# Linear attention in front of a mixture-of-experts layer: who turns the rows, who centres them, and the order of a batch's steps

## The chip, the cores and the metric

The kernel runs on one core of one Trainium2 chip. Its metric is the device time in microseconds (us) of one execution. The engines run side by side, each with its own instruction queue, and wait for each other on semaphores: TensorE (PE: products, and transposes by product), VectorE (DVE), ScalarE (ACT), GpSimd (POOL) and SyncE (SP, which here only issues DMAs).

## The reference

The input x holds 16 batches of 1024 tokens of width 256. After a layer norm, two branches are added to x:

```python
xn = _layernorm(x, axis=-1)
Q = _feature_map(xn @ Wq.T + bq)      # elu(t) + 1, 16 heads of 16
K = _feature_map(xn @ Wk.T + bk)
V = xn @ Wv.T + bv
KV = jnp.einsum('bshd,bshe->bhde', K, V)
K_sum = K.sum(axis=1)
Z = 1.0 / (jnp.einsum('bshd,bhd->bsh', Q, K_sum) + 1e-06)
out = jnp.einsum('bshd,bhde,bsh->bshe', Q, KV, Z) @ Wo.T + bo
```

The second branch is an expert layer: softmax gate scores, the best 256 tokens of each batch for each of 8 experts, two products with a gelu between, and the weighted rows added back at their tokens.

## The kernel before

There are two stages. The second, the expert layer (lines 1342 to 1704), is the same in both kernels but for the shape of one helper. The change is in the first, the attention.

**Stage one, batch by batch.** Batch n has 8 tiles j of 128 tokens. DVE takes the statistics (`stats_of`, `moments_of`), POOL adds epsilon and raises to the power -1/2 (`norm`), DVE scales (`root_of`). Each tile is centred into `xm` (`centre`, on DVE, line 899), split into two fp16 halves, a high one on ACT (`high`) and a low one on DVE (`low`), both in `xhl`. The tile must then lie with its width on the partitions: `turn` on PE makes four 128x128 transposes into PSUM (line 1157), and ACT copies them to `xT` (`turn_out`, line 734). `project` is the bias product and six products for K and V into `pP`, then six narrow ones for the gate into `pG`. ACT takes K's negative part, the copy `kv1`, and the exponential `ek`; DVE joins them into `phik`; `sum_kv` adds the tile to the running K-V sums in `pKV`. `q_part` makes a quarter u of the queries; DVE takes its negative part (`q_negative`, line 931), ACT its exponential, and DVE joins them (`q_feature`).

**The second half of a batch's work** comes two batches later, m = n - 2, inside the same eight steps: `blocks_of` on POOL masks the sums by head, `denominators` on PE, then a chain on DVE, `shift` (adds 1e-6), `invert` (a reciprocal and a first bf16 part) and `split_rest` (two more parts, `zpart`); `reciprocals` on PE spreads the parts over four quarters u (line 1233), `divide` on DVE multiplies each with the queries (line 964), `turn_kv` and `fold_o` fold the output weights into `mo`, `output` on PE makes the result (line 1247) and `add_x` on DVE adds it to the rows (line 971) to which POOL has added the output bias (`add_bo`, line 672).

**What sets the order.** No scheduler: each engine's loop body lists, for each step j from 0 to 7, what is issued there, and each queue is taken strictly in that order. On PE:

```python
if j < NT - 1:
    turn(n, j + 1)
...
project(n, j)
...
if j == 3:
    reciprocals(m, 0)
...
    if j > 0:
        sum_kv(n, j - 1)
```

A quarter's product is at steps 4, 5 and 7 and at the end. From batch 5 to 15 DVE also runs the selection of the best 256 tokens for the first four batches, one of three operations over 512 columns at each step (`top_slot`); in batches 0 to 7 it reads four blocks of expert weights for their largest value (`piece`, at odd steps, line 976), which SP loads into `stage`. SP's body issues these loads, the loads of x for two uses (`xring`, `x2ring`), the store of `xhl` into `table`, zeros into `acc` and the stores of the result into `mix`.

After batch 15 a tail finishes batches 14 and 15, and the first gathers of the expert layer are issued.

## Time and profile before

| | us |
|---|---|
| median of 3 runs | 2110.15 |
| lowest and highest | 2107.7, 2118.55 |
| profiled execution, its own time | 2106.6 |
| its span, first to last instruction | 2104.9 |
| first stage to the last tile of batch 15 | about 671 |
| tail between the stages | 42.7 |
| expert layer | 1391.3 |

The profile is one execution. A group of instructions has a line of the kernel, an engine, what it writes and reads, the shape, a count, the busy time, and the idle time before it with what ended it. PE's matmuls are pipelined, so that the durations of neighbours overlap; what one costs its queue is the distance to the next start. The cuts of the stretches below are at the starts of batches 2, 5 and 8 on PE and at the end of batch 15. "PEclk" is the clock granted to TensorE as a share of full speed.

### The profile page before, as it was taken

Reading aid. Unit: us, or ns where it says so; the run is one execution under the profiler, and the core shown is the slowest. Engines: PE = TensorE matmul, PEld = TensorE weight load, DVE = VectorE, ACT = ScalarE, POOL = GpSimd, SP = SyncE. Lnnn points to the kernel's source line nnn. Section 1 sums busy time; section 2 is a strip of 40 time slices with the busy share of each in tenths; the row PEclk is TensorE's granted clock in tenths of the full one; section 3 lists DMA queues with packets and bytes.
Section 4 is the critical chain, followed back from the end, with each engine's and each line's share of the span. In section 5 each row is a group of like instructions: output and inputs, shape, how many; then the busy total and the mean of one; then the engine's idle time right before and its main releaser. Section 6 shows DMA issues by size and latency. Waiting matters only on the chain.

```text
span 2104.9 us, 40792 instructions
## 1 busy us (share of the span) xinstructions
PE 1960.8 (93%) x14240; PEld 1328.3 (63%) x14240; DVE 1392.8 (66%) x2836; ACT 1247.0 (59%) x1975; POOL 881.1 (42%) x776
## 2 busy tenths in 40 slices
PE   4899988898999899999999999999999999999974
PEld 2566656666666566666666666666666666666653
DVE  5877888778786477775567877555555555555535
ACT  3855555566565266566666666666666666666642
POOL 2122112312221356464545554556454545555532
PEclk9999999999999899999999999999999999999987
DMA  5565555334433455555566666666666666666676
GB/s 161 170 200 162 165 176 158 113 124 128 151 131 111 114 121 125 125 125 132 117 160 161 152 172 154 169 153 176 152 166 167 168 165 159 159 168 169 165 181 190
DMA packets 379402, 321.61 MB, mean 153 GB/s; under 512 B 155013, under 2 KB 360842, under 8 KB 379274
## 3 DMA queue, kind: packets, MB, share of 16 engines
q1 hardware_dynamic: 312842, 236.00, 37.5%
q0 software_dynamic: 49152, 67.14, 17.0%
q10 hardware_dynamic: 17280, 16.78, 2.4%
q8 instruction: 78, 1.28, 0.2%
q14 instruction: 50, 0.41, 0.1%
HBM read 185.61 MB, written 100.66 MB: 136 GB/s over the span
## 4 chain that ended last, share of the span: by engine, by line
PE 55%; DMA 3%; POOL 3%; SPq 2%; DVE 2%; issue 1%; ACT 1%; POOLq 0%; ACTq 0%; DVEq 0%
PE pY L1673 27%; PE pH L1659 27%; POOL acc L1499 2%; SPq L223 2%; DMA stage<-in_w 1%; DMA xg<-table,idx 1%; POOL xg L217 1%; DVE yo L1574 1%; DMA lacc<-acc 0%; DVE hid L1561 0%; DMA acc<-yo,idx 0%; DVE w2s L205 0%; ACT hid L1519 0%; ACT w2s L197 0%; ACT gel L1516 0%
## 5 line engine op out<-in xcount | busy, mean ns | idle before, releaser
L1673 PE MATMUL pY<-w2s,hid 128*128 128x256 f16 x6144 | 756.6, 273 | 16.8 <-DVE hid L1561 16.8
L1659 PE MATMUL pH<-xgT,w1s 128*128 128x512 f16 x3072 | 750.3, 381 | 4.3 <-PEq L319 4.3
L1673 PEld LDWEIGHTS pY<-w2s,hid 128*128 128x128 f16 x6144 | 600.3, 98 | 199.9 <-DVE hid L1561 20.8
L1499 POOL DMA_INDIRECT acc<-yo,idx x256 | 415.0, 1621 | 549.3 <-DVE yo L1574 490.8
L1561 DVE SCALAR_TENSOR_TENSOR hid<-gel,cur,hid 128x512 f16<-128x512 f32 x512 | 382.4, 747 | 379.8 <-ACT hid L1519 371.2
L1516 ACT ACTIVATE gel<-pH,cur 128x512 f32<-128x512 f32 x512 | 350.0, 684 | 396.2 <-PE pH L1659 386.5
L1659 PEld LDWEIGHTS pH<-xgT,w1s 128*128 128x128 f16 x3072 | 301.4, 98 | 261.1 <-issue 9.4
L1519 ACT ACTIVATE hid<-gel,cur 128x512 f16<-128x512 f32 x512 | 369.7, 722 | 16.6
L217 POOL DMA_INDIRECT xg<-table,idx x256 | 281.4, 1099 | 113.4 <-issue 60.6
L1169 PE MATMUL pP<-wkv,xT 128*128 128x512 f16 x768 | 190.6, 385 | 0.0
L672 POOL TENSOR_TENSOR x2ring<-x2ring,bo_all 128x512 f32 (+1 forms) x64 | 85.2, 1361 | 151.6 <-DMA x2ring<-in_x 151.5
L205 DVE SCALAR_TENSOR_TENSOR w2s<-stage,cur,w2s 128x1024 f16<-128x1024 f32 x64 | 82.7, 1294 | 82.2 <-ACT w2s L197 82.1
L642 POOL TENSOR_SCALAR veps<-moments 128x8 f32<-128x8 f32 x16 | 3.9, 243 | 314.9 <-DVE moments L836 314.9
L1574 DVE TENSOR_SCALAR yo<-pY,gains,cur 128x256 f32<-128x256 f32 x256 | 121.5, 536 | 13.0 <-PE pY L1673 11.3
L1169 PEld LDWEIGHTS pP<-wkv,xT 128*128 128x128 f16 x768 | 76.4, 99 | 83.6 <-issue 5.4
L1247 PE MATMUL pO<-mo,qz 128*128 128x256 f32 x480 | 117.0, 386 | 6.4 <-DVE qz L964 4.9
L205 DVE SCALAR_TENSOR_TENSOR w1s<-stage,cur,w1s 128x1024 f16<-128x1024 f32 x64 | 82.5, 1290 | 57.9 <-ACT w1s L197 57.8
L773 ACT ACTIVATE ek<-pP,winv_neg 128x256 f32<-128x256 f32 x128 | 59.9, 468 | 90.0 <-PE pP L1169 90.0
L197 ACT ACTIVATE w2s<-stage,cur 128x1024 f16<-128x1024 f32 x64 | 72.8, 1139 | 62.1 <-DMA stage<-in_w 62.0
L734 ACT ACTIVATE xT<-pTK 128x512 f16<-128x512 f16 x128 | 75.8, 592 | 48.7 <-PE pTK L1157 47.2
L1247 PEld LDWEIGHTS pO<-mo,qz 128*128 128x128 f32 x480 | 87.4, 190 | 21.3 <-DVE qz L964 7.9
L1187 PE MATMUL pKV<-kv,phik 128*128 128x129 f32 x512 | 86.9, 293 | 11.5 <-DVE phik L1086 11.5
(185 smaller groups left out, 1995.9 us busy)
## 6 DMA issues: line engine op xcount, KB each, us to landing
stage<-in_w SPq DMA_DIRECT2D x160, 512.0 KB, 5.1
xring<-in_x SPq DMA_DIRECT2D x16, 1024.0 KB, 7.0
x2ring<-in_x SPq DMA_DIRECT2D x16, 1024.0 KB, 9.0
table<-xhl SPq DMA_DIRECT2D x32, 512.0 KB, 3.9
acc<-zeros SPq DMA_DIRECT2D x16, 1024.0 KB, 7.0
mix<-x2ring SPq DMA_DIRECT2D x32, 512.0 KB, 2.8
fmix<-mix SPq DMA_DIRECT2D x48, 256.0 KB, 5.9
facc<-acc SPq DMA_DIRECT2D x48, 256.0 KB, 6.6
```

The lines of the kernel that those rows point to most:

```text
L205: nc.vector.scalar_tensor_tensor(out=part_dst(i, 1, r), in0=staged(r), scalar=cur[i][:, 2 + r // 2:3 + r // 2], in1=part_dst(i, 0, r), op0 ...
L217: nc.gpsimd.indirect_dma_start(xg[i][:, s, :, :, :].rearrange("p a c t -> p (a c t)"), None, table, bass.IndirectOffsetOnAxis(ap=idx[q % 4 ...
L1169: last = t.matmul(pP[j % 2][:, :], xT[h][:, a, c, cols], wkv[:, b, c, :], start=False, stop=k == 2 and c == DC - 1)
L1187: last = t.matmul(pKV[:, c * (P + 1):(c + 1) * (P + 1)], phik[:, j % 2, c * P:(c + 1) * P], kv1[:, j % 2, DC + c, :], start=j == 0 and c = ...
L1247: last = t.matmul(bank[:, i, :], qz[h][:, c, tokens], mo[:, c, :], start=c == 0, stop=c == DC - 1)
L1499: g.indirect_dma_start(acc, bass.IndirectOffsetOnAxis(ap=idx[q][:, s:s + 1], axis=0), yo[i][:, s, :], None, compute_op=ALU.add).then_inc(a ...
L1516: a.activation(gel[:, hc % 2, :], pH[hc % 4][:, :], ACT.Gelu_apprx_tanh, scale=c[:, 0:1]).then_inc(gel_done, 1)
L1519: a.activation(hid[:, hc % 4, 0, :], gel[:, hc % 2, :], ACT.Copy, scale=c[:, 1:2]).then_inc(hhi_done, 1)
L1561: v.scalar_tensor_tensor(out=hid[:, hc % 4, 1, :], in0=gel[:, hc % 2, :], scalar=cur[(q // 2) % 2][:, 1:2], in1=hid[:, hc % 4, 0, :], op0= ...
L1574: last = v.tensor_scalar(yo[i][:, s, :], pY[s // 2][:, s % 2, :], gains[:, ds((b * 4 + q) * 4 + s, 1)], cur[(q // 2) % 2][:, 4:5], ALU.mul ...
L1659: last = t.matmul(pH[hc % 4][:, :], w[:, aw, c, hc * P:(hc + 1) * P], xgT[i][:, ad, c, :], start=k == 0 and c == 0, stop=k == 2 and c == D ...
L1673: last = t.matmul(pY[s // 2][:, s % 2, :], hid[:, hc % 4, ad, s * P:(s + 1) * P], w[:, aw, hc, :], start=hc == 0 and k == 0 and s % 2 == 0 ...
```

## The change

- The rows are turned by SP, with a transposing DMA from `xhl` to `xT` for each tile, in place of PE's four transposes and ACT's copy. It waits for the tile's low half, and at the first tile of a half of the batch for the gate products of the batch before (`gated`), the last readers of that half of `xT`.
- POOL centres the tiles, four `xm` buffers ahead in place of two.
- The gate products of a tile come one step later, the K-V sums two steps behind (`phik` and `kv1` have four buffers).
- The chain of the denominators is spread: `shift` on ACT after step 0, `invert` at step 1 on DVE, `split_rest` at 2, `divide` at 4, 5, 5 and 6; PE has the quarters' products at 2, 3, 6 and 7. The bank that held the transposes, now `pE`, serves the denominators, two of the four quarters of `reciprocals`, and one `output`.
- ACT takes the copies of the sums, of `kvT` and of `dd`, and the queries' negative part, straight from PSUM. The key and query numbers are the same; for the queries the 1 of the feature map is added through the bias and the join is a maximum.
- In the tail, batch 15's chain is taken in between batch 14's output and the weight splits, and the first gathers stand ahead of the last `add_bo`.

```diff
-def turn_probs(pe, k, bank, tiles):
-for t, jl in enumerate(tiles):
-    last = nc.tensor.transpose(bank[0:2 * rows_of(k), t * P:(t + 1) * P], probs[:, jl, lane_cols(k)], ident[:, :])
+def turn_probs(pe, k, bank):
+for jl in range(HALF):
+    last = nc.tensor.transpose(bank[0:2 * rows_of(k), jl * P:(jl + 1) * P], probs[:, jl, lane_cols(k)], ident[:, :])
 last.then_inc(p_turned, 1)
...
-    dve.wait_ge(rows_done, at(rows_done, k + 1))
+    dve.wait_ge(rows_done, at(rows_done, k))
...
-pK = pTK[:, 1, :].bitcast(F32)
+pE = ps("pE", [P, 512])
 pP = [ps(f"pP{i}", [P, 512]) for i in range(2)]
 pG = ps("pG", [P, 2, HALF, 64])
 pKV = ps("pKV", [P, 512])
 pQ = ps("pQ", [P, 512])
...
-banks_z, banks_o, banks_mo = {True: [pD], False: [pD, pKV]}, {True: [pO], False: [pO, pG]}, {True: pD, False: pP[0]}
+banks_z = {True: [pE, pD, pE, pD], False: [pD, pKV, pD, pKV]}
...
+    def turn(n, j):
+        h, jj = divmod(j, HALF)
+        value = held(sp, at(lo_done, n, j))
+        sp.wait_ge(consts, 1)
+        sp.wait_ge(lo_done, value)
+        if jj == 0 and not (isinstance(n, int) and n == 0):
+            value = held(sp, at(gated, n - 1, h))
+            sp.wait_ge(consts, 1)
+            sp.wait_ge(gated, value)
+        sp.dma_start_transpose(
+            xT[h][:, :, :, jj * P:(jj + 1) * P].rearrange("p a c t -> p (a c) t"),
+            xhl[h][:, jj, :, :, :].rearrange("p a c t -> p (a c t)")).then_inc(x_turned[j], 16)
+
...
+    def body(n, s1, s2, load, load2, scan, nxt):
+        m = n - LAG
+        if s1:
+            turn(n, HALF)
+            store_rows(n, 0)
...
         if s1:
+            turn(n, HALF + 1)
+        if load2:
...
+        if s1:
+            turn(n, HALF + 2)
+            turn(n, HALF + 3)
+            store_rows(n, 1)
+        if scan:
+            pieces(n, range(2, PIECES))
+        if nxt:
+            turn(n + 1, 0)
+            turn(n + 1, 1)
+        if s1:
...
+        if nxt:
+            turn(n + 1, 2)
         if s2:
...
+            store_mix(m, 0)
+        if nxt:
+            turn(n + 1, 3)
+        if s2:
+            store_mix(m, 1)
...
+    for j in range(HALF):
+        turn(0, j)
...
+    def centre(n, j):
+        if j == 0:
+            pool.wait_ge(aggr_done, at(aggr_done, n))
+        if n > 0 or j >= HALF:
+            pool.wait_ge(lo_done, at(lo_done, n, j - HALF))
+        g.tensor_scalar(xm[:, j % HALF, :], xring[:, n % XR, j, :], moments[:, j, 0:1], None, ALU.subtract).then_inc(xm_done, 1)
...
+    for n in range(NB):
+        for j in range(HALF, NT):
+            centre(n, j)
+        if n >= LAG:
             for u in range(4):
...
+                add_bo(n - LAG, u)
+        if n < NB - 1:
             norm(n + 1)
...
+            for j in range(HALF):
+                centre(n + 1, j)
+        if n + 1 >= LAG:
+            blocks_of(n + 1 - LAG)
...
-    def turn_out(n, j):
-        h, jj = divmod(j, HALF)
-        act.wait_ge(turned, at(turned, n, j))
-        if jj == 0:
-            act.wait_ge(q_proj, at(q_proj, n, 2 * h + 1 - 4))
-        a.activation(xT[h][:, :, :, jj * P:(jj + 1) * P], pT[:, :, :, :], ACT.Copy).then_inc(xT_done, 1)
-
...
+    def queries(n, u):
         c = u % DC
         act.wait_ge(q_proj, at(q_proj, n, u))
         act.wait_ge(q_done, at(q_done, n, u - 2))
-        a.activation(qraw[:, u % 2, :], banks_q[mixed][u][:, :], ACT.Identity, scale=winv[:, 0:1], bias=bqT[:, c:c + 1]).then_inc(qraw_done, 1)
...
+        a.activation(qraw[:, u % 2, :], pQ[:, :], ACT.Identity, scale=winv[:, 0:1], bias=bqT_one[:, c:c + 1]).then_inc(qraw_done, 1)
         act.wait_ge(qneg_done, at(qneg_done, n, u))
         a.activation(eq[:, u % 2, :], eq[:, u % 2, :], ACT.Exp, scale=-1.0).then_inc(eq_done, 1)
...
+    def sums_out(n):
+        act.wait_ge(kv_used, at(kv_used, n, NT - 1))
+        a.activation(kvring[:, n % QR, :, :].rearrange("p c t -> p (c t)"), pKV[:, 0:DC * (P + 1)], ACT.Copy).then_inc(kv_out, 1)
+
+    def shift(m):
+        act.wait_ge(den, at(den, m))
+        a.activation(dd[:, :], pE[:, 0:P], ACT.Identity, bias=eps[:, 0:1]).then_inc(shifted, 1)
...
+    for n in range(NB):
+        m, s2, nxt = n - LAG, n >= LAG, n < NB - 1
...
+            if j < HALF:
+                high(n, j + HALF)
+            elif nxt and j > HALF:
+                high(n + 1, j - HALF)
+            keys(n, j)
...
+            project(n, j)
+            if j > 0:
+                gate(n, j - 1)
             if s2:
                 if j == 0:
-                    pe.wait_ge(qraw_done, at(qraw_done, n, -2))
                     denominators(m)
...
                     turn_kv(m)
                 if j == 2:
                     fold_o(m)
+            if j in (2, 3):
+                q_part(n, j - 2)
...
+            if s2:
                 if j == 3:
                     reciprocals(m, 0)
                 if j == 4:
                     reciprocals(m, 1)
+                    reciprocals(m, 2)
                 if j == 5:
-                    reciprocals(m, 2)
+                    reciprocals(m, 3)
+                    output(m, 0)
                 if j == 6:
...
+                    output(m, 1)
                 if j == 7:
...
+                    output(m, 2)
+            if n == PREP and j == 6:
...
+                q_part(n, j - 4)
+            if j >= 2:
+                sum_kv(n, j - 2)
+        gate(n, NT - 1)
+        sum_kv(n, NT - 2)
         if s2:
             output(m, 3)
...
+        sum_kv(n, NT - 1)
```

How the order moves, on PE, step 3 and the start of step 4 of a batch (`pP`: K and V of a tile, `pG`: gate, `pKV`: sums, `pQ`: a quarter of the queries, `pTK`: turned rows). Before:

```order
L1157 MATMUL pTK<-ident,xhl 128x128 [waits xT_done,lo_done]
L1157 MATMUL pTK<-ident,xhl 128x128 x3
L1165 MATMUL pP<-bias_rows,bias_lhs 128x512 [waits kv_done,xT_done]
L1169 MATMUL pP<-wkv,xT 128x512 x6
L1176 MATMUL pG<-wg,xT 128x8 x6
L1233 MATMUL pD<-zpart,spread 128x128 [waits zsplit,mo_done]
L1233 MATMUL pD<-zpart,spread 128x128 x11
L1187 MATMUL pKV<-kv,phik 128x129 [waits kv_done,k_done]
L1187 MATMUL pKV<-kv,phik 128x129
```

The same step on PE now, with what follows it in step 4 and the start of step 5:

```order
L1168 MATMUL pP<-bias_rows,bias_lhs 128x512 [waits kv_done,x_turned3]
L1172 MATMUL pP<-wkv,xT 128x512 x6
L1184 MATMUL pG<-wg,xT 128x8 x6
L1209 MATMUL pQ<-xT,wq 128x512 [waits qraw_done]
L1209 MATMUL pQ<-xT,wq 128x512 x5
L1236 MATMUL pE<-zpart,spread 128x128 [waits zsplit]
...
L1236 MATMUL pD<-zpart,spread 128x128 [waits mo_done]
L1236 MATMUL pD<-zpart,spread 128x128 x11
L1236 MATMUL pE<-zpart,spread 128x128 [waits qz_done]
```

The turning is gone from the queue, a quarter of the queries stands ahead of the first spread of the reciprocals, and two further spreads follow at step 4, the second of them waiting for DVE's first `divide`.

On DVE, from the end of step 3 to the first `divide` of step 5, in a batch with selection (`qring`: the joined queries, `qz`: the divided ones). Before:

```order
L964 TENSOR_TENSOR qz<-qring,pD 128x512 [waits bcast]
L1086 SCALAR_TENSOR_TENSOR phik<-kv,ek 128x256 [waits ek_done,kv_used,kv_done]
L892 TENSOR_SCALAR rstd<-rpow 128x8 [waits rpow_done,lo_done]
L906 SCALAR_TENSOR_TENSOR xhl<-xm,rstd,xhl 128x256 [waits hi_done,rstd_done]
L248 MAX_INDEX topu<-topv,rows 64x8 [waits found]
L906 SCALAR_TENSOR_TENSOR xhl<-xm,rstd,xhl 128x256 [waits hi_done]
L899 TENSOR_SCALAR xm<-xring,moments 128x256 [waits lo_done]
L971 TENSOR_TENSOR x2ring<-x2ring,pO 128x512 [waits out_mm,bo_done]
L964 TENSOR_TENSOR qz<-qring,pD 128x512 [waits bcast]
```

The same place on DVE now:

```order
L997 TENSOR_TENSOR qz<-qring,pE 128x512 [waits bcast]
L968 TENSOR_TENSOR qring<-qraw,eq 128x512 [waits eq_done,qraw_done]
L948 TENSOR_REDUCE gmax<-pG 128x4 [waits gated]
L950 TENSOR_TENSOR gsub<-pG,gmax 128x32 [waits gmax_done]
L934 TENSOR_SCALAR rstd<-rpow 128x8 [waits rpow_done,lo_done]
L941 SCALAR_TENSOR_TENSOR xhl<-xm,rstd,xhl 128x256 [waits hi_done,rstd_done]
L248 MAX_INDEX topu<-topv,rows 64x8 [waits found]
L975 SCALAR_TENSOR_TENSOR phik<-kv,ek 128x256 [waits ek_done,kv_used,kv_done]
L997 TENSOR_TENSOR qz<-qring,pD 128x512 [waits bcast]
L997 TENSOR_TENSOR qz<-qring,pE 128x512 [waits bcast]
```

Between the first `divide` and the second there now stand the join of a query quarter, the gate's maximum, the scale of the next batch and a low half that waits for ACT.

On SP, the start of a batch with weight blocks (`stage`). Now (before, `stage` was the first issue of the body, with no wait for a low half):

```order
L526 DMA_TRANSPOSE xT<-xhl 128x4x128 [waits gated,consts]
...
L537 ISA [waits row_out0,consts]
L537 DMA table<-xhl 128x4x512
...
L515 ISA [waits piece_done0,consts]
L515 DMA stage<-in_w 128x1024
...
L566 DMA xring<-in_x 128x8x256
...
L526 DMA_TRANSPOSE xT<-xhl 128x4x128 [waits lo_done,consts]
```

The block's load now stands behind a turn and a store, and both of those behind the low half of tile 4.

## Rows read from the trace of the kernel before

**Rows 1.** The page's first part: engine, busy us (share of the span), instructions.
```profile
PE 1960.8 (93%) x14240; PEld 1328.3 (63%) x14240; DVE 1392.8 (66%) x2836; ACT 1247.0 (59%) x1975; POOL 881.1 (42%) x776
```

**Rows 2.** By stretch: us, each engine's busy us, then PEclk, DMA share, GB/s.
```profile
34.00:92.80 58.80, 51.72 (x386) 30.61 (x384) 44.70 (x131) 45.70 (x97) 11.12 (x13) 1.00 0.49 154
92.80:215.80 123.00, 112.96 (x938) 77.61 (x935) 96.73 (x242) 73.78 (x154) 27.26 (x33) 0.99 0.54 172
215.80:345.70 129.90, 115.60 (x934) 79.37 (x932) 109.02 (x280) 73.66 (x154) 29.02 (x33) 0.96 0.54 171
345.70:671.00 325.30, 299.94 (x2491) 205.48 (x2492) 253.20 (x704) 194.83 (x406) 74.64 (x87) 0.99 0.41 131
671.00:713.70 42.70, 30.77 (x240) 26.07 (x232) 24.83 (x52) 6.17 (x9) 16.40 (x20) 0.83 0.39 117
713.70:2105.00 1391.30, 1345.04 (x9248) 904.97 (x9248) 846.87 (x1379) 846.58 (x1149) 713.36 (x566) 0.98 0.62 155
```

**Rows 3.** PE in order of time, batch 12: start us, us, what [idle before].
```profile
511.14 0.39 PE L1157 MATMUL pTK<-ident,xhl 128*128 128x128 f16 x4
511.36 0.38 PE L1165 MATMUL pP<-bias_rows,bias_lhs 128*128 128x512 f16 x1
...
516.88 0.71 PE L1187 MATMUL pKV<-kv,phik 128*128 128x129 f32 x4 [0.45 <-DVE phik L1086]
...
519.78 1.13 PE L1258 MATMUL pD<-woT,kvT 128*128 128x256 f32 x4 [0.32 <-DVE kvT L1092]
...
525.20 0.83 PE L1233 MATMUL pD<-zpart,spread 128*128 128x128 bf16 x12 [1.98 <-DVE zpart L957]
525.87 0.66 PE L1187 MATMUL pKV<-kv,phik 128*128 128x129 f32 x4
...
528.43 0.31 PE L1176 MATMUL pG<-wg,xT 128*128 128x8 f16 x6 [0.16 <-DVE gsub L915]
...
551.50 0.38 PE L1165 MATMUL pP<-bias_rows,bias_lhs 128*128 128x512 f16 x1
```

**Rows 4.** Waits of PE, 92.8 to 671: total us, times, longest.
```profile
PE pD L1233 <- DVE zpart L957: 30.6, 14, 3.1
```

**Rows 5.** One line of the kernel each: duration ns min/median/max, first and last start.
```profile
L734 ACT ACTIVATE xT<-pTK x128: 573/597/605, 32.7 to 656.3; 128x512 f16<-128x512 f16 x128
...
L899 DVE TENSOR_SCALAR xm<-xring,moments x128: 331/344/1364, 27.6 to 641.5; 128x256 f32<-128x256 f32 x128
...
L906 DVE SCALAR_TENSOR_TENSOR xhl<-xm,rstd,xhl x128: 454/468/1545, 28.9 to 644.7; 128x256 f16<-128x256 f32 x128
...
L964 DVE TENSOR_TENSOR qz<-qring,pD x60: 669/687/690, 106.9 to 701.3; 128x512 f32<-128x512 f32 x60
```

**Rows 6.** Groups by shape, 511.4 to 551.5: busy us, mean ns, idle before.
```profile
L1086 DVE SCALAR_TENSOR_TENSOR phik<-kv,ek 128x256 f32<-128x256 f32 x8 | 3.7, 465 | 2.4 <-ACT ek L782 2.4
...
L937 DVE SCALAR_TENSOR_TENSOR qring<-qraw,eq 128x512 f32<-128x512 f32 x4 | 2.7, 684 | 0.0
...
L740 ACT ACTIVATE qraw<-pQ,bqT,winv 128x512 f32<-128x512 f32 x3 | 2.3, 772 | 0.6 <-PE pQ L1207 0.6
...
L248 DVE FIND_INDEX8 topu<-topv,rows 64x8 uint32<-64x512 f32 x3 | 2.0, 676 | 0.0
...
L915 DVE TENSOR_TENSOR gsub<-pG,gmax 128x32 f32<-128x32 f32 x2 | 0.4, 191 | 0.1
```

**Rows 7.** DVE, then POOL at the same moment, in order of time (batch 6).
```profile
288.81 1.54 DVE L906 SCALAR_TENSOR_TENSOR xhl<-xm,rstd,xhl 128x256 f16<-128x256 f32 x1
...
288.81 5.50 POOL L672 TENSOR_TENSOR x2ring<-x2ring,bo_all 128x512 f32 x4 [14.11 <-DMA x2ring<-in_x]
```

**Rows 8.** Transposing DMAs on SP's queue (ns as in rows 5); a load's landing.
```profile
L223 SPq DMA_TRANSPOSE xgT<-xg x256: 1189/1262/5297, 694.1 to 2033.8; - x128
...
xring<-in_x SPq DMA_DIRECT2D x16, 1024.0 KB, 7.0
```

**Rows 9.** The tail on PE in order of time: start us, us, [idle before].
```profile
694.86 1.61 PE L1258 MATMUL pP<-woT,kvT 128*128 128x256 f32 x4 [3.57 <-DVE kvT L1034]
```

More of the change, by code:

```diff
@@ L433, in block_program @@
             row_out = [event(f"row_out{h}", step=16, credit=1) for h in range(2)]
-            turned = event("turned", per=NT, credit=HALF + 1)
-            xT_done = event("xT_done", per=NT, credit=1)
+            x_turned = [event(f"x_turned{j}", step=16, credit=1) for j in range(NT)]
             proj = event("proj", per=NT)
@@ L970, in add_x @@
                     tiles = x2ring[:, ds(m % 2, 1), 2 * u:2 * u + 2, :].rearrange("p o j d -> p (o j) d")
-                    v.tensor_tensor(tiles, tiles, pair(banks[u % len(banks)]), ALU.add).then_inc(mix_done, 1)
+                    v.tensor_tensor(tiles, tiles, pair(banks_o[not alone][u]), ALU.add).then_inc(mix_done, 1)
                 def piece(n, q):
```

549 lines of the change are left out of this document (238 added, 311 removed).

## The prediction

> **What bounds the kernel now.** I read the page's first part, then the busy time by stretch, then PE in order of time within one batch, then its waits. PE is busy for 93% of the span [rows 1], but the share hides three regimes [rows 2]. The expert layer, 1391.3 us, is not touched, so the change can only work on the first 714 us. There, the first two batches take 58.8 us, batches 2 to 4 take 123.0 (41.0 each), batches 5 to 7 take 129.9 (43.3 each), batches 8 to 15 take 325.3 (40.7 each), and a tail takes 42.7. The reader should see that in batches 5 to 7 DVE is busy for 109.0 of 129.9 us, where the selection and the weight blocks fall together, and in the others for about 78%. So PE bounds most batches, with DVE close behind in three of them.
>
> Batch 12 on PE runs from 511.36 to 551.50, 40.14 us [rows 3]. In it stand four waits with a row, 0.45, 0.32, 1.98 and 0.16, in sum 2.9. The longest is the first spread of the reciprocals, which waits for the last part of the denominator chain on DVE: all 14 batches have it, in sum 30.6 us, up to 3.1 at once [rows 4]. The rest of the batch, 37.2 us, is PE's queue itself.
>
> **The change part by part.**
>
> *Turning leaves PE.* The four transposes of a tile start at 511.14 and the next product at 511.36: 0.22 us of queue [rows 3]. Eight per batch are 1.8 us. What is left of PE's own queue is 37.2 - 1.8 = 35.4 us per batch. No product is added. This is the floor.
>
> *ACT.* It loses eight copies of 0.60 (4.8 us per batch) [rows 5] and gets four more passes over a query quarter at about 0.77 (3.1) [rows 6], plus three copies that DVE had. Its sum hardly moves from 73.8 us in three batches, some 25 each [rows 2], far under 35. At nothing, covered by PE's queue.
>
> *DVE.* It loses eight centrings of 0.34 (2.8) [rows 5], four negative parts and three small copies. With these it falls from 109.0 / 3 = 36.3 us per batch in batches 5 to 7 [rows 2] to about 31, and elsewhere to about 27. It is not the bound by its sum, but it can be by its order.
>
> *The spread chain.* The reciprocals' parts are made at steps 1 and 2 and used at the end of step 3, behind a query quarter: the 1.98 goes. What is late next is the pair of banks. PE puts three spreads close together, and the fourth needs the second `divide`. Between the end of the first `divide` and the end of the second, DVE now has the query join 0.68, three short operations of 0.19, a low half 0.47, a selection step 0.68, a key join 0.47 and the `divide` 0.69 [rows 5, 6]: 3.6 us, and the low half first waits for ACT's high half of the tile, some 0.7 with the two hand-overs, so 4.3. PE in the same time has a spread, 0.67 from start to start [rows 3], K-V sums, a tile's projection and gate: from 525.20 to 528.43 before, less 0.22 of turning, is 3.0. So a new wait of 1.3, and I add 0.5 for the small waits of 0.16 to 0.45 that the order doesn't remove. A batch with selection alone then takes 35.4 + 1.3 + 0.5 = 37.2 us.
>
> In batches 2 to 4 there is no selection step in that list, so the new wait is 0.6; blocks of weights add to DVE elsewhere. I take 37.0. In batches 5 to 7 both are there. A block's reduction at step 3 stands straight ahead of the first `divide`, and that one at step 1 now waits for a load that SP issues only after a turn and a store, where it was first. I take 2 us more than 37.2: 39.2.
>
> *Centring on POOL.* It adds eight operations of 128x256 with one tensor input. No row has such a one. Above it stands POOL's two-input one over 128x512, 5.50 / 4 = 1.37 [rows 7]; below it DVE's own 0.34 [rows 5]. I take 0.7, half of the upper for half the columns. POOL was busy for 27.3 us in three batches [rows 2], 9.1 each, and comes to 15 of 37: no bound, four tiles ahead. Its price is paid on DVE. Where POOL adds the bias, DVE's low half took 1.54 in place of its median 0.47 [rows 5, 7], while `divide`, with one input in PSUM, never took more than 0.69 in 60 [rows 5]. So the operations with two inputs in SBUF wait for POOL. This is in the 0.5 above for the average; the upper bound is a rival.
>
> The Trainium skill has this as a rule ("SBUF — State Buffer", section "SBUF: two separate sides"): a DVE operation with two SBUF inputs and a GpSimd operation that reads SBUF take an exclusive lock on the shared port for a whole instruction. The trace agrees, 1.54 beside 1.37. By it the new centrings, which read SBUF, block as the bias sums do.
>
> *Turning by DMA.* Eight issues per batch on SP, 1.26 us each at the median of the expert layer's, which have the same shape [rows 8]: 10.1 us of SP's queue in 37. SP has otherwise some eight issues a batch; it has room. The trace doesn't show when one lands. Below, it is the issue itself, 1.3 us; above, the issue and a whole 1 MB load in front of it, 7.0 [rows 8], so 8.3, and with two loads in front 15. PE wants a tile about a half batch after its low half, some 18 us, except for tile 3: its low half comes at step 7 and the first query quarter wants it at step 2. Between lie PE's end of the batch and two steps, about 12 us. Only a zero fill and one store stand ahead. At nothing, then, with the upper bound as a rival.
>
> Against this speaks a rule of the Trainium skill ("VectorE: DVE Perf Modes", sections "The three transpose paths" and "Rules for kernel authors"): a 128x128 transpose costs 390 ns on TensorE and 1309 ns by DMA, and TensorE is to be used where PSUM will do. By it a tile of four would take 5.2 us by DMA. The trace differs on both: four in 0.22 us of PE's queue, and an issue for four in 1.26.
>
> *Start.* The first tile could start some 3 us earlier, since four centrings are made at once, but the first weight block now waits behind four turns and holds DVE at step 1. Between 4 us gained and 4 lost I take nothing.
>
> *Tail.* PE waited 3.57 us for a copy of batch 15 that stood behind two weight splits on DVE [rows 9]. ACT has that copy now, and the chain is made earlier. The last bias sums still stand behind eight gathers. I take 4 us of 42.7, between 0 and 8.
>
> **Sum.** Batches 2 to 15 took 123.0 + 129.9 + 325.3 = 578.2. Now 3 x 37.0 + 3 x 39.2 + 8 x 37.2 = 526.2, so 52.0 less, and 4 in the tail: 56. The profiled execution took 2106.6, its span 2104.9, so 2050.6 for it. The median of the runs shown is 3.5 higher. I say 2050. The granted clock was 0.96 to 0.99 in these stretches [rows 2]; what was lost at the lower level after a wait is part of the times before, and I count no further gain for it.
>
> **The rivals.**
>
> *PE's floor is reached.* If DVE's list does not hold up the fourth spread, 14 batches take 35.4: 495.6, a gain of 82.6, and 4: 2020. For it: the waits that I add are made of hand-overs that I only estimate. Against it: DVE's list at step 4 has eight entries, one of them waiting for ACT.
>
> *POOL holds DVE.* Eight more POOL operations per batch fall among twenty DVE ones with two SBUF inputs. If two of them a batch on the way to a `divide` or a key join wait a further 1.1 (1.54 less 0.47), the batches take 2.2 us more, 31 in 14: 2081. For it: the row of 1.54. Against it: most centrings come right after the low half that frees their buffer, while DVE goes on to other work.
>
> *No change.* The order is looser on PE but PE meets new waits at every step, of the sort between 0.3 and 0.5: 4 us a batch give back all, 2106. Only if several at once.
>
> *Transposes land late, slower.* Tile 3's must land 12 us after its low half. If DMAs with 512 small rows wait in their rings behind zeros, a store, `table` and `xring`, and SP stands at the store of the result until DVE has added it, each batch waits for what exceeds 12 us. It decides from 4 us beyond, where the 3.7 us gained per batch are gone; at 18 us after the low half, 6 us of wait, the 14 batches come out 2.3 us longer each: 2106.6 + 32 - 4 = 2135. For it: the longest of the 256 issues took 5.3 us [rows 8]. Against it: the DMA share is 0.54 and 0.41 [rows 2].
>
> **How the numbers follow.** A measurement of this kernel can tell some 0.5% from no change, 10.5 us. The forecast has 0.50, by itself 2038 to 2066; PE's floor 0.20; POOL 0.18; no change 0.06; late transposes 0.06. That leaves out a range from 2022 to 2088 hardly more than the last two and a part of the floor. Faster by more than 0.5%: 0.50 + 0.20 + 0.18 and a part of the rest, 0.89; the same 0.06; slower 0.05.
>
> **What would show it.** PE's first product of a batch should come every 37 us, 39 in batches 5 to 7. The first spread should have no wait for the last denominator part, and the fourth one about 1.3 for `divide`. No wait of PE for a transposing DMA beyond the first batches, and issues of about 1.26 on SP. POOL's centrings between 0.34 and 1.37, and DVE's low halves in two groups, near 0.47 and above 1. The tail should have no 3.57 before its fold. The forecast is wrong if PE's waits name DMAs, if DVE is busy for over 90% of a batch, or if the expert layer moves from 1391.3 us.

## The result, and the profile after

The changed kernel takes 2033.1 us at the median of four runs (2030.8 to 2034.3), beside 2112.6 for the kernel before in runs on the same chip: 0.962 of it, 95% interval 0.959 to 0.965. I had said 2050, between 2022 and 2088. The profiled execution's span went from 2104.9 to 2032.5 us, 72.4 less.

The page's first part, as in [rows 1]:

```profile
PE 1913.8 (94%) x13728; PEld 1289.4 (63%) x13728; DVE 1311.2 (65%) x2598; ACT 1229.0 (60%) x1959; POOL 1025.3 (50%) x904
```

The stretches of [rows 2], cut at the same batches (the columns are those of [rows 2]):

```profile
31.40:89.60 58.20, 51.19 (x320) 28.20 (x321) 37.46 (x112) 43.79 (x93) 28.97 (x32) 0.90 0.89 222
89.60:199.90 110.30, 105.09 (x841) 70.98 (x840) 80.46 (x193) 70.52 (x151) 56.67 (x61) 1.00 0.84 226
199.90:317.40 117.50, 105.99 (x837) 71.37 (x835) 94.20 (x236) 70.25 (x150) 56.51 (x58) 0.99 0.78 215
317.40:600.90 283.50, 277.18 (x2254) 189.34 (x2255) 216.04 (x590) 184.85 (x396) 141.85 (x144) 1.00 0.64 177
600.90:636.60 35.70, 25.36 (x232) 21.30 (x221) 21.56 (x44) 7.04 (x12) 16.67 (x20) 1.00 0.48 148
636.60:2032.50 1395.90, 1345.48 (x9248) 904.92 (x9248) 847.27 (x1379) 846.69 (x1149) 711.40 (x565) 0.98 0.63 154
```

| stretch | before | after | gain | forecast |
|---|---|---|---|---|
| batches 0 and 1, with the start | 92.8 | 89.6 | 3.2 | 0 |
| batches 2 to 4 | 123.0 | 110.3 | 12.7 | 12.0 |
| batches 5 to 7 | 129.9 | 117.5 | 12.4 | 12.3 |
| batches 8 to 15 | 325.3 | 283.5 | 41.8 | 27.7 |
| tail | 42.7 | 35.7 | 7.0 | 4 |
| expert layer | 1391.3 | 1395.9 | -4.6 | 0 |

Batch 12 on PE, in order of time, beside [rows 3]:

```profile
460.13 0.38 PE L1168 MATMUL pP<-bias_rows,bias_lhs 128*128 128x512 f16 x1
...
470.70 1.46 PE L1209 MATMUL pQ<-xT,wq 128*128 128x512 f16 x6
471.99 0.83 PE L1236 MATMUL pE<-zpart,spread 128*128 128x128 bf16 x12
...
475.49 0.83 PE L1236 MATMUL pE<-zpart,spread 128*128 128x128 bf16 x12
...
478.18 0.29 PE L1184 MATMUL pG<-wg,xT 128*128 128x8 f16 x6
479.13 0.84 PE L1236 MATMUL pD<-zpart,spread 128*128 128x128 bf16 x12 [0.66 <-DVE qz L997]
...
495.32 0.38 PE L1168 MATMUL pP<-bias_rows,bias_lhs 128*128 128x512 f16 x1
```

The batch takes 35.19 us in place of 40.14. The first spread has no wait. A single one is left, 0.66 us ahead of the fourth. DVE around it, from the first `divide` to the second:

```profile
473.41 0.67 DVE L997 TENSOR_TENSOR qz<-qring,pE 128x512 f32<-128x512 f32 x1
474.36 0.69 DVE L968 TENSOR_TENSOR qring<-qraw,eq 128x512 f32<-128x512 f32 x1 [0.27 <-ACT eq L782]
...
476.74 0.74 DVE L941 SCALAR_TENSOR_TENSOR xhl<-xm,rstd,xhl 128x256 f16<-128x256 f32 x1 [1.24 <-ACT xhl L762]
...
477.48 0.68 DVE L248 FIND_INDEX8 topu<-topv,rows 64x8 uint32<-64x512 f32 x1
478.08 0.40 DVE L975 SCALAR_TENSOR_TENSOR phik<-kv,ek 128x256 f32<-128x256 f32 x1
478.40 0.67 DVE L997 TENSOR_TENSOR qz<-qring,pD 128x512 f32<-128x512 f32 x1
```

The first `divide` ends at 474.08, the second at 479.07, and the spread starts at 479.13. PE's waits from batch 1 to the end of batch 15, beside [rows 4] (total us, times, longest):

```profile
PE pE L1236 <- DVE qz L997: 11.6, 7, 2.5
PE pD L1236 <- DVE qz L997: 7.1, 10, 1.3
PE pKV L1195 <- DVE phik L975: 4.2, 3, 2.8
PE pE L1236 <- DVE zpart L991: 3.5, 4, 1.2
```

The 30.6 us for `zpart` have become 3.5; waits for `qz`, the divided queries, have come, 18.7 us in all. What had no row before are POOL's centring and SP's turns (ns as in [rows 5]):

```profile
L683 POOL TENSOR_SCALAR xm<-xring,moments x128: 914/925/1481, 26.3 to 560.4; 128x256 f32<-128x256 f32 x128
```

```profile
L526 SPq DMA_TRANSPOSE xT<-xhl x128: 1188/1197/3917, 28.6 to 577.3; - x128
...
  PE pP L1168: 21.7, 2
...
DMA to landing us min/median/max: 2.4/4.0/9.6
```

PE waited for a turned tile twice: 18.9 us at the very start, where it has nothing else to do, and 2.76 us in batch 0. DVE, from the start of the first batch to the end of batch 15, waited for the weight blocks (total us, times, longest):

```profile
DVE piece_max L1008 <- DMA stage<-in_w: 35.7, 13, 5.4
```

### The profile page after: what moved, and what is told of

The parts are those of the page before. It is cut to its first block, busy times and chain, and to the rows that moved or that the text cites. A ratio compares the mean times of both kernels' runs of the same rounds, so it can differ in the third digit from the quotient of the medians.

```text
span 2032.5 us, 39422 instructions
## 1 busy us (share of the span) xinstructions
PE 1913.8 (94%) x13728; PEld 1289.4 (63%) x13728; DVE 1311.2 (65%) x2598; ACT 1229.0 (60%) x1959; POOL 1025.3 (50%) x904
## 4 chain that ended last, share of the span: by engine, by line
PE 56%; DMA 3%; POOL 3%; issue 2%; DVE 2%; SPq 2%; ACT 1%; POOLq 0%; ACTq 0%; DVEq 0%
PE pY L1674 28%; PE pH L1660 28%; POOL acc L1500 2%; SPq L223 2%; DMA stage<-in_w 2%; DMA xg<-table,idx 1%; POOL xg L217 1%; DVE yo L1575 1%; DVE hid L1562 0%; DMA acc<-yo,idx 0%; ACT hid L1520 0%; DVE lmix L1593 0%; ACT gel L1517 0%; DMA lacc<-acc 0%; POOL idx L212 0%
## 5 line engine op out<-in xcount | busy, mean ns | idle before, releaser
L1674 PE MATMUL pY<-w2s,hid 128*128 128x256 f16 x6144 | 757.2, 273 | 22.0 <-DVE hid L1562 18.7
L683 POOL TENSOR_SCALAR xm<-xring,moments 128x256 f32<-128x256 f32 x128 | 130.6, 1031 | 82.4 <-DVE xhl L941 75.4
L1575 DVE TENSOR_SCALAR yo<-pY,gains,cur 128x256 f32<-128x256 f32 x256 | 121.5, 536 | 12.7 <-PE pY L1674 11.0
L197 ACT ACTIVATE w1s<-stage,cur 128x1024 f16<-128x1024 f32 x64 | 72.9, 1140 | 51.0 <-DMA stage<-in_w 50.8
L673 POOL TENSOR_SCALAR veps<-moments 128x8 f32<-128x8 f32 x16 | 12.9, 807 | 175.9 <-DVE moments L875 175.9
L941 DVE SCALAR_TENSOR_TENSOR xhl<-xm,rstd,xhl 128x256 f16<-128x256 f32 x128 | 63.5, 496 | 58.1 <-ACT xhl L762 58.1
L1209 PE MATMUL pQ<-xT,wq 128*128 128x512 f16 x384 | 93.3, 379 | 0.8 <-ACT qraw L780 0.8
L712 POOL TENSOR_TENSOR x2ring<-x2ring,bo_all 128x512 f32<-128x512 f32 x64 | 88.5, 1413 | 5.0 <-DMA x2ring<-in_x 5.0
```

The source lines that it names most:

```text
L197: nc.scalar.activation(part_dst(i, 0, r), staged(r), ACT.Copy, scale=cur[i][:, 2 + r // 2:3 + r // 2]).then_inc(whi_done, 1)
L683: g.tensor_scalar(xm[:, j % HALF, :], xring[:, n % XR, j, :], moments[:, j, 0:1], None, ALU.subtract).then_inc(xm_done, 1)
L1575: last = v.tensor_scalar(yo[i][:, s, :], pY[s // 2][:, s % 2, :], gains[:, ds((b * 4 + q) * 4 + s, 1)], cur[(q // 2) % 2][:, 4:5], ALU.mul ...
L1674: last = t.matmul(pY[s // 2][:, s % 2, :], hid[:, hc % 4, ad, s * P:(s + 1) * P], w[:, aw, hc, :], start=hc == 0 and k == 0 and s % 2 == 0 ...
```

## The experiments

"2 to 4" and "5 to 7" are us per batch, "12" is batch 12, each from the profiled execution, from PE's first product of a batch to that of the next. The ratio is to runs of the kernel before on the same chip, whose medians were 2108.7 to 2112.6; so two kernels measured on different chips can differ by some 4 us for that alone.

| kernel | median us | ratio, 95% interval | 2 to 4 | 5 to 7 | 12 |
|---|---|---|---|---|---|
| before | 2112.6 | | 41.0 | 43.3 | 40.1 |
| after | 2033.1 | 0.962 (0.959 to 0.965) | 36.8 | 39.2 | 35.19 |
| turn_only | 2135.2 | 1.013 (1.011 to 1.014) | 45.8 | 45.5 | 40.6 |
| turn_clear | 2100.9 | 0.996 (0.994 to 0.998) | 41.6 | 42.4 | 40.7 |
| chain_late | 2041.8 | 0.969 (0.968 to 0.971) | 38.3 | 40.7 | 35.18 |
| late_swap | 2053.8 | 0.973 (0.970 to 0.976) | 40.9 | 42.3 | 35.23 |
| one_behind | 2053.9 | 0.975 (0.973 to 0.976) | 38.7 | 39.2 | 36.10 |
| centre_dve | 2038.9 | 0.967 (0.965 to 0.970) | 37.8 | 39.4 | 35.00 |
| centre_twice | 2054.4 | 0.975 (0.972 to 0.977) | 37.0 | 39.5 | 35.75 |
| pieces_first | 2010.5 | 0.954 (0.950 to 0.958) | 34.5 | 36.4 | 35.19 |
| picks_moved | 2026.6 | 0.961 (0.958 to 0.964) | 36.4 | 38.9 | 34.37 |
| first_moved | 2003.1 | 0.949 (0.947 to 0.952) | 34.6 | 35.8 | 34.37 |
| both | 2014.0 | 0.954 (0.951 to 0.956) | 34.6 | 36.3 | 34.37 |
| scales_late | 2006.1 | 0.952 (0.950 to 0.954) | 34.5 | 35.7 | 34.37 |

**turn_only: the turning alone, in the kernel before.**

```diff
-                                turn(n, j + 1)
...
-                                turn_out(n, j + 1)
...
+                    if s1:
+                        turn(n, HALF)
+                        store_rows(n, 0)
                     if scan:
                         pieces(n, range(2))
...
-                pe.wait_ge(xT_done, at(xT_done, n, j))
+                pe.wait_ge(x_turned[j], at(x_turned[j], n))
```

> The kernel before, with the turning alone taken over by SP's transposing DMA (PE's four transposes and ACT's copy gone, nothing else moved). My theory: PE's queue loses 0.22 us at each of 128 tiles, 28 us in all, but the three of them that stand between the denominators and the first spread only lengthen the wait for the last denominator part, which DVE's chain sets, and batches 5 to 7 are held by DVE. So 1.1 us per batch in 13 batches and nothing in three: about 2098 us beside 2113, and PE's wait for zpart grows from 30.6 to some 38 us. Rival 1, turning is worth its whole queue: 28 us, 2084. Rival 2, the transposing DMAs land late where SP has other loads: PE waits for x_turned and the time stays at 2113 or rises.

It was slower, by 26 us. PE did not wait for turned tiles beyond the start (rival 2 names the wrong wait); its waits for `zpart` went to 55.6 us. DVE in batch 4, then PE's wait over the first stage:

```profile
198.99 0.42 DVE L1116 COPY kvT<-pD 128x256 f32<-128x256 f32 x1
203.93 1.22 DVE L1000 TENSOR_REDUCE piece_max<-stage 128x1 f32<-128x1024 f32 x1 [4.53 <-DMA stage<-in_w]
...
207.52 0.92 DVE L971 RECIPROCAL zz<-dd 128x128 f32<-128x128 f32 x1
```

```profile
PE pD L1248 <- DVE zpart L981: 55.6, 13, 7.4
```

The weight block's load stood behind a turn on SP, the block's reduction waited for it, and the chain of the denominators stands behind the reduction. In batch 12 there are no blocks, the turns' 1.8 us are gone from the queue, and nothing is gained (40.6 in place of 40.1). PE there:

```profile
557.22 0.83 PE L1248 MATMUL pD<-zpart,spread 128*128 128x128 bf16 x12 [2.20 <-DVE zpart L981]
...
558.65 2.77 PE L1184 MATMUL pP<-wkv,xT 128*128 128x512 f16 x6
```

The wait is 2.20 in place of 1.98, and the six products behind it take 2.77 us; the clock granted over this batch is 0.96 of full speed, a part of it at the lower level (1.2 of 2.4 GHz). In batch 12 of the kernel before they took 1.46 in this place:

```profile
526.81 1.46 PE L1169 MATMUL pP<-wkv,xT 128*128 128x512 f16 x6
```

**turn_clear: turn_only with the loads first.**

```diff
+                    if scan:
+                        pieces(n, range(2))
                     if s1:
                         turn(n, HALF)
                         store_rows(n, 0)
-                    if scan:
-                        pieces(n, range(2))
```

> The kernel before with DMA turning alone, as in turn_only, but SP issues the first two weight blocks of a batch ahead of the turn of tile 4 and the store, as the kernel before did. My theory: turn_only came out 26 us above before because in batches 0 to 7 block 0's load stood behind that turn, so that DVE waited up to 5.4 us for it at step 1, ahead of the denominator chain (PE's wait for zpart went to 6 to 7 us a batch). With the load first these waits go, some 4 to 5 us in each of six batches: 2105 to 2111 us, batches 2 to 4 at 40 to 41.5 and not 45.8, and PE's longest wait for zpart at 3 to 4 us. Rival: it is the turning itself (late landings, or a lower clock after each longer wait) that costs it: then the time stays above 2125.

```profile
91.90:216.70 124.80, 110.89 (x840) 73.50 (x839) 97.34 (x243) 61.22 (x130) 27.27 (x33) 0.96 0.69 199
```

34 us back, and 4 us under the lowest that I expected: batches 2 to 4 took 137.5 in turn_only. The cause of turn_only's loss is the load, not the turning. Turning alone in the kernel before is worth 8 us, 0.4%, and not the 28 of its queue, and in the profiles batches 2 to 15 give only 1.8 of it (577.8 and 576.0 us). The traces show where the queue time went: PE's listed waits there grew from some 49 to 63 us, the one for `zpart` from 30.6 to 34.1, and PE ran for longer at the lower clock (0.96, 0.95 and 0.97 granted in batches 2 to 4, 5 to 7 and 8 to 15, beside 0.99, 0.96 and 0.99 [rows 2]). Two neighbouring batches of turn_clear, 11 and 12, wait the same 2.20 us at the first spread:

```profile
469.23:508.80 39.57, 35.25 (x281) 23.73 (x279) 32.61 (x90) 20.27 (x44) 9.45 (x11) 1.00 0.59 160
508.80:549.48 40.68, 36.76 (x281) 24.36 (x279) 32.45 (x90) 20.38 (x44) 9.46 (x11) 0.96 0.53 156
```

The second had a stretch at the lower clock (mean 0.96), and took 1.1 us longer. No run puts the turning back on PE in the changed kernel, where little waiting is left to cover it; what it is worth there was not measured.

**chain_late: the chain in one piece at step 3.**

```diff
-                        if s2 and j == 1:
-                            invert(m)
...
-                            if j == 2:
+                            if j == 3:
+                                invert(m)
                                 split_rest(m)
```

> The changed kernel with the denominator chain not spread: the reciprocal and the two further parts both at DVE's step 3, in place of steps 1 and 2. My theory: the first spread waits for zpart again, by 1.5 to 2.5 us in each of 14 batches: 2054 to 2068 us beside 2033, and the wait for zpart stands in PE's list with 20 to 35 us. Rival: the query quarter that now stands ahead of the first spread (2 us of PE's queue) covers it, less than 0.5 us per batch, up to 2040; then the spreading as such was worth little and the order on PE did it.

8.7 us slower, less than I gave it, and all of it in batches 2 to 7. In batch 12 the last part starts on DVE and the first spread on PE here:

```profile
479.19 0.29 DVE L991 TENSOR_TENSOR zpart<-zrest,zpart 128x128 bf16<-128x128 f32 x1
```

```profile
480.51 0.83 PE L1235 MATMUL pE<-zpart,spread 128*128 128x128 bf16 x12
```

It is ready at 479.48, 1.0 us early. The quarter ahead of the spread, 1.3 us of queue, covers it. The rival holds for batches 8 to 15.

**late_swap: chain_late, and the first spread ahead of the quarter.**

```diff
-                        if j in (2, 3):
-                            q_part(n, j - 2)
+                        if j == 2:
+                            q_part(n, 0)
...
                             if j == 3:
                                 reciprocals(m, 0)
...
+                        if j == 3:
+                            q_part(n, 1)
```

> The changed kernel with the denominator chain not spread (as in chain_late) and, on PE at step 3, the first spread ahead of the query quarter. chain_late showed the last denominator part ready 1.0 us before the first spread in batch 12; the quarter is 1.3 us of queue. My theory: the two edits cover each other; without both the first spread waits again, by 0.3 us in batches 8 to 15 and by 1.3 us more than in chain_late in batches 2 to 7: about 2053 us. Rival 1: a clock drop behind the new wait or a knock-on adds to it, 1 us more a batch, above 2060. Rival 2: the wait only changes place (the quarter stood still behind the divide), 2042 as chain_late.

2053.8, as expected, with PE's wait for `zpart` back (batches 1 to 15):

```profile
PE pE L1235 <- DVE zpart L991: 33.4, 13, 5.5
```

But in batch 12 that wait is only 0.20 us, and the batch takes 35.23. So most of the 1.98 of [rows 3] went there with neither the spreading nor the quarter. What is left as its cause is DVE's shorter list and the rest of the new order; that is argued, and no run separates them.

**one_behind: the K-V sums one step behind.**

```diff
-                        if j >= 2:
-                            sum_kv(n, j - 2)
+                        if j >= 1:
+                            sum_kv(n, j - 1)
                     gate(n, NT - 1)
-                    sum_kv(n, NT - 2)
```

> The changed kernel with the K-V sums one step behind in place of two. My theory: the sum of a tile then meets phik half a microsecond early at most steps, as it did before the change (0.45 us in one step of batch 12), 0.5 to 1.5 us per batch: 2041 to 2055 us beside 2033. Rival: a tile's product with a gate and a quarter between give ACT and DVE time enough at each step, no wait for phik of over 0.2 us, 2033.

21 us slower, at the far end of what I expected. PE's waits for `phik` over batches 1 to 15, which were 4.2 us:

```profile
PE pKV L1195 <- DVE phik L975: 37.1, 25, 5.7
```

**centre_dve: centring back on DVE.** The calls of `centre` move from POOL's list into DVE's as well.

```diff
-                    g.tensor_scalar(xm[:, j % HALF, :], xring[:, n % XR, j, :], moments[:, j, 0:1], None, ALU.subtract).then_inc(xm_done, 1)
+                    v.tensor_scalar(xm[:, j % HALF, :], tile_of(n, j), moments[:, j, 0:1], None, ALU.subtract).then_inc(xm_done, 1)
```

> The changed kernel with the centring back on DVE (four buffers kept). My theory: DVE gets eight more operations of 0.34 us per batch, 2.7 us. In batches 5 to 7, where DVE is busy for 94.2 of 117.5 us, they cost nearly whole, 8 us; in the others two or three of them stand between the divides and cost 0.3 to 0.6 us per batch, 5 us: about 2046 us beside 2033. Rival, the lock between POOL and DVE is what the centring costs: without POOL's 128 centrings DVE's slow low halves (up to 1.61 us) go, and the time stays at 2033 or falls.

5.8 us slower by the medians, but its four runs go from 2032.4 to 2046.0, so that the size is uncertain. In the profile batches 2 to 4 lose 3.2 us; batches 5 to 7, where I expected 8, lose 0.6, and in batch 12 DVE's centring is the faster by 0.2. Taking eight operations off DVE is worth some 7% of the change's gain.

**centre_twice: each centring done twice.**

```diff
+                    g.tensor_scalar(xm[:, j % HALF, :], ..., ALU.subtract).then_inc(xm_once, 1)
+                    pool.wait_ge(xm_once, at(xm_once, n, j))
                     g.tensor_scalar(xm[:, j % HALF, :], ..., ALU.subtract).then_inc(xm_done, 1)
```

> The changed kernel with each centring on POOL done twice into the same tile (a wait between the two), DVE's work unchanged. It doubles the suspected cost of POOL beside DVE. My theory: POOL's price is small, since centre_dve moved batches 10 to 14 by only 0.2 us and the low halves that wait for POOL are off the divides; POOL comes to some 23 us of 35, and the centred tile comes 1.1 us later at each tile: 2033 to 2042 us, batches 10 to 14 within 0.5 of 35.19. Rival: the shared port holds DVE for about 1 us each time the two meet; with eight more meetings a batch some two of them stand ahead of a divide or a key join, 2 us a batch, 2060 us or more.

21 us slower, between the two. Batch 12 cost 0.56, about as my theory has it. Batches 0 and 9 cost 12 together, which neither theory had: new there are waits of PE for ACT's copy `kv`, up to 2.3 us, and what makes that copy late is open. What the doubled POOL work adds to DVE's operations is small: the mean low half went from 0.50 to 0.52 us over all 128.

**pieces_first: the two loads ahead of the turn, in the changed kernel.** The edit is that of turn_clear.

> The changed kernel with the first two weight blocks issued by SP ahead of the turn of tile 4 and the store of rows. My theory: DVE's waits for the blocks (28.7 us in all, batches 0 to 7) fall by half, and batches 2 to 7 lose a part of their waits at the third and fourth spread, 0.5 to 1.5 us each: 2024 to 2030 us beside 2033. Rival: 1 MB of weights ahead of the turn makes the turned rows late; PE waits for x_turned in batches 0 to 7 and the time is 2033 or more.

22.6 us faster, where I had expected 3 to 9. The stretches as in [rows 2], then DVE's wait for the blocks:

```profile
31.90:83.00 51.10, 48.10 (x321) 27.04 (x322) 38.93 (x113) 43.89 (x93) 28.76 (x33) 0.95 1.05 253
83.00:186.50 103.50, 103.50 (x840) 70.93 (x838) 80.04 (x193) 69.50 (x150) 56.57 (x60) 1.00 0.92 240
186.50:295.60 109.10, 104.17 (x837) 70.81 (x836) 93.99 (x236) 69.92 (x150) 56.57 (x58) 1.00 0.85 232
```

```profile
DVE piece_max L1008 <- DMA stage<-in_w: 11.9, 5, 3.5
```

Batches 2 to 4 are PE's queue alone, busy for 103.5 of 103.5 us.

**picks_moved: the selection step off the divides.**

```diff
-                        top_slot(n, j)
+                        for i in {0: (0,), 1: (1,), 2: (2,), 5: (3,), 6: (4, 5), 7: (6,)}.get(j, ()):
+                            top_slot(n, i)
...
+                    top_slot(n, NT - 1)
```

> The changed kernel with the selection step that stands between the first and the second divide moved behind the divides (steps 3 and 4 of the selection to DVE's steps 5 and 6). My theory: the fourth spread's wait of 0.66 us is this 0.75 us operation; without it batches 8 to 15 take 34.5 and not 35.2, and batches 5 to 7 some 0.7 less each: 2033 less 7 is 2026. Rival: DVE's low half there waits for ACT's high half, or the operation only delays another join, and PE's batch stays at 35.2: 2033.

The total is as expected, in part by luck. Batches 8 to 15 give 4.2 us in the profile, but batches 5 to 7 only 0.6 of the 2 that I had for them, the start is 2.3 slower, and the expert layer, which the edit doesn't touch, was 6.8 shorter than in the changed kernel's profile. What the edit does is clear in batch 12, which starts and ends here, with no wait between, 34.38 us later:

```profile
459.49 0.38 PE L1170 MATMUL pP<-bias_rows,bias_lhs 128*128 128x512 f16 x1
...
477.69 0.83 PE L1238 MATMUL pD<-zpart,spread 128*128 128x128 bf16 x12
...
493.87 0.38 PE L1170 MATMUL pP<-bias_rows,bias_lhs 128*128 128x512 f16 x1
```

So a wait with 0.66 in its row cost 0.82.

**first_moved: both edits.**

> The changed kernel with both: the first two weight blocks issued ahead of the turn, and the selection step between the divides moved behind them. The two runs apart gave 2010.5 and 2026.6 us, PE's batch without a listed wait 34.37 us. My theory: the two gains add up where they meet other batches: batches 8 to 15 go from 35.19 to 34.4 (5 us less than 2010.5), batches 5 to 7 from 36.35 to some 35.5, since the block's reduction at step 3 still stands ahead of the first divide (2.5 us): about 2003 us. Rival: they overlap, since with the loads early DVE's list is no longer the limit anywhere but in the expert-layer part: 2008 to 2010.

2003.1, the fastest version found, 0.949 of the kernel before and 30 us under the changed one. Its batches 5 to 7:

```profile
186.80:294.10 107.30, 104.15 (x836) 70.81 (x836) 92.72 (x234) 70.17 (x150) 56.48 (x58) 1.00 0.87 236
```

**both: the reductions moved as well.**

```diff
-                        pieces(n, range(2, PIECES))
+                        pieces(n, (2,))
...
+                    if scan:
+                        pieces(n, (3,))
...
-                        if n < PIECE_NB and j % 2 == 1:
-                            piece(n, j // 2)
+                        if n < PIECE_NB and j in (1, 6, 7):
+                            piece(n, max(j - 5, 0))
...
+                    if n < PIECE_NB:
+                        piece(n, 3)
```

> As first_moved, and in addition the blocks' reductions on DVE moved off the divides (to steps 1, 6, 7 and the end of a batch, with SP's loads of the third and fourth block moved to match). My theory: batches 2 to 7 then reach the floor of 34.4 as well, 2 us less each in batches 5 to 7 than 36.35: about 1999 us. Rival: the fourth block's load, now late in a batch, meets the store and makes DVE wait at the batch's end, 1 to 3 us in each of batches 0 to 7: 2005 to 2015.

My theory fell. Batches 5 to 7 got slower by 0.5 us each than in first_moved, and batch 1 took 30.1 in place of 24.6. The rival's time is right, its mechanism is not: DVE's wait for the blocks is down to 1.3 us in all, and most of what made batch 1 long is PE's wait for a turned tile:

```profile
PE pP L1174 <- DMA xT<-xhl: 3.8, 1, 3.8
```

In first_moved it was 0.5 in that batch. Of the 12.8 us between the two profiles, 6.0 lie in the expert layer, which no edit touches.

**scales_late: first_moved, and the weight scales at the end of batch 9.**

```diff
-                    if n == PIECE_NB + 1:
-                        weight_scales()
...
                             q_feature(n, 2)
+                            if n == PIECE_NB + 1:
+                                weight_scales()
...
-                    if n == PIECE_NB + 1:
-                        weight_scales()
```

> first_moved with the scales of the expert weights (some ten small DVE operations ahead of step 0 of batch 9) moved to step 7 of the same batch, behind the divides and two of the additions. In the changed kernel and in first_moved batch 9 took 37.5 and 37.9 us beside a floor of 34.4. My theory: these operations hold the chain of joins at the start of the batch; behind the divides they fall where DVE waits for others, batch 9 comes to 34.4 to 35.5, and the whole to 2000 us beside 2003. Rival: they hold what follows as much at the batch's end (the last joins and the first K-V sums of batch 10), batches 9 and 10 stay 3 us over the floor in sum and the time at 2003.

A miss: batches 9 and 10 took 39.2 and 35.0 us in place of 37.9 and 34.4, with a new wait of 1.79 us for `phik`. The rival is the nearer: the two batches stay 5.4 us over the floor in sum, and 2006.1 can't be told from 2003.1.

## Why the prediction was right where it was, and wrong where it was

*The total, 2050: 2033.1.* It lies in the range that I gave, but below the 2038 to 2066 of the forecast by itself, and not by the rival of PE's floor either, whose condition (DVE holds up no spread) did not come true: PE still waits 18.7 us for the divides. The profiled execution took 2034.3 where I had 2050.6. By the table above these 16 us are 14.1 in batches 8 to 15, 3.2 at the start, 3.0 in the tail and 0.8 in batches 2 to 7, less 4.6 in the expert layer.

*PE's floor, 35.4: mis-sized, 34.37.* This is the largest error, the floor itself wrong by 1.0 us in each batch that reaches it. I took the listed idle time, 2.9 us, from the batch, and 0.22 for each turning. But a wait costs more than its row (0.82 for 0.66 in picks_moved), and the rows of batch 12 before show why:

```profile
515.86 0.29 PE L1176 MATMUL pG<-wg,xT 128*128 128x8 f16 x6
516.01 0.42 PE L1252 MATMUL pD<-ident,kvm 128*128 128x128 f32 x2
...
542.03 0.39 PE L1157 MATMUL pTK<-ident,xhl 128*128 128x128 f16 x4
542.49 1.99 PE L1247 MATMUL pO<-mo,qz 128*128 128x256 f32 x8
```

The gate products have 0.29 by their row, but the next group starts 0.15 after them. Ahead of a wait the row's whole 0.29 is counted as work, so 0.14 of the wait is hidden; ahead of the four listed waits it is 0.14 to 0.17 each, 0.6 in sum. At 542.03 four transposes hold the queue for 0.46 in place of 0.22, with no wait listed behind them: 0.24 more. Some 0.2 of the 1.0 stays open. So of the 4.95 us that batch 12 gained, 2.0 are the transposes, 3.5 the four old waits in full, and 0.8 were lost again to the new one. Beside its wait batch 12 shows 34.5, 0.9 less than 35.4, and 8 x 0.9 = 7 us is half of the 14 that I missed in batches 8 to 15.

*The new wait at the fourth spread, 1.3: right place, half the size, 0.66.* DVE took 4.99 us from divide to divide where I had 4.3 (low half behind ACT's high half: 1.24 and 0.74). But I counted PE's time from the end of the first divide; PE started the third spread only 1.41 us after it, at 475.49, and its work from there took the 3.0 that I had. That picks_moved removes the wait shows that the selection step decides it. The 0.5 that I added for small waits wasn't there. With the floor this is 0.9 + 0.64 + 0.5 = 2.0 per batch, 37.2 forecast and 35.2 measured.

*The 1.98 at the first spread goes: right, for a partly wrong reason.* In batches 2 to 7 it goes by the spread chain and the quarter (chain_late, late_swap); in batch 12 it is nearly gone without either (0.20 left in late_swap).

*Batches 5 to 7, 39.2: the number right, the mechanism as I named it, the sizes by luck.* The load behind a turn and a store held DVE; with the load first they take 36.4, so it cost 2.8 where I had 2 for it and the block's reduction together. Moving the selection step as well takes 0.6 (first_moved, 35.8), and 1.4 over the floor of 34.4 is left. These are 4.8 on 34.4 where I had 3.8 on 35.4. In batches 2 to 4 I had 37.0 and got 36.8, but for a floor of 34.4 and not 35.4: the same load cost 2.2 there, where I had named no cost for it but 0.6 at the spread and a vague rest. Two errors cancelled. At the start I weighed it and took nothing; in the changed kernel it cost 7 us (58.2, and 51.1 in pieces_first).

*The engines' sums: right.* DVE is busy for 31.4 us per batch in batches 5 to 7 and 27.0 in batches 8 to 15, where I had 31 and 27.

*Turning: at nothing on SP and no wait of PE, right.* The issue took 1.20 us at the median (forecast 1.26), landing 4.0 and never over 9.6, inside the 12 us that I allowed. The rival of late transposes fell. The Trainium skill's figure for the DMA ("VectorE: DVE Perf Modes", section "The three transpose paths", 1309 ns each, so an estimate of 5.2 us for four) lies between the median and the longest; its advice to keep to TensorE would have cost only 8 us in the kernel before (turn_clear), because the queue time saved came back as longer waits for DVE and time at the lower clock. That is the worth of turning alone and not its worth in the changed kernel.

*Centring on POOL, 0.7: mis-sized, 0.93* and 1.03 at the mean. It changed nothing, as POOL was under 60% busy: 18 to 19 us per batch where I had 15. The rival that POOL holds DVE fell: `divide` never took over 0.69, and centre_twice shows less than 0.6 us per batch in batch 12. The mean low half was 0.53 us before and 0.50 after, and of 128 low halves 6 took over 0.7 us and one over 1, where I had looked for a group above 1. One operation with two inputs in SBUF did get longer, the join of the query quarters:

```profile
L968 DVE TENSOR_TENSOR qring<-qraw,eq x64: 673/686/1754, 45.4 to 599.0; 128x512 f32<-128x512 f32 x64
```

Its mean went from 0.68 to 0.85 us. It is 0.71 in centre_dve but 0.74 in centre_twice, so it doesn't grow with POOL's work, and its cause is open.

*Tail, 4: 7.0.* The 3.57 wait before the fold is gone, as said; the granted clock of the tail was 0.83 before [rows 2] and 1.00 after. New waits for the divides stand there (2.26 and 1.64 us); the gain was not taken apart further.

*The clock: no gain counted, but one was in the sum.* The granted clock went from 0.99, 0.96 and 0.99 [rows 2] to 1.00, 0.99 and 1.00 in batches 2 to 15. My 37.2 was built from batch 12, which ran at 1.00, so that the forecast had this gain without naming it.

*Expert layer.* It was to stay, and I had named its moving as a sign of being wrong. It took 4.6 us more in this profile. Between the same two products it took 5.6 more than before here, but -1.8 to 3.3 in all other kernels with the same expert layer and 5.5 in one. It goes with no edit; I don't explain it.

## What to carry to other kernels

A listed wait can understate what it costs on a pipelined engine (here 0.66 for 0.82), so read the floor from a stretch without waits. When a queue that issues loads gets new work with waits of its own, follow every load that now stands behind it to who reads it and what is queued behind the reader: here that cost more (34 us in the kernel before, 23 in the changed one) than the turning alone gained (8). An operation taken off an engine that waits in that place anyway lengthens the wait, and pays only once the wait's other end has moved too.
